# The last message pass of a four-layer graph network: VectorE's adds and scans in another order, marks of going-on destinations made once

## The chip, the cores and the metric

One core of one Trainium2 chip runs the whole kernel in one launch. The metric is the device time of a launch in microseconds (us), as the median of a few runs. Engines are named as the profile names them: PE is TensorE (PEld its weight loads), DVE is VectorE, ACT is ScalarE, POOL is GpSimd, SP is SyncE, which issues most DMAs here.

## The reference, cut to what matters

Four graph layers run over the same 106,250 edges, sorted by destination, and 6,250 nodes of 128 features; a layernorm follows each. The change lies in the last layer, an attention whose softmax is taken per destination and per feature:

```
a = f_src[src] + f_dst[dst]
e = where(a >= 0, a, 0.2 * a)
seg_max = segment_max(e, dst)                 # per destination and feature
ex = exp(e - seg_max[dst])
sa = ex / segment_sum(ex, dst)[dst]
rst = segment_sum(f_v[src] * sa, dst)
x = layernorm(x + rst)
```

## The kernel before

Nodes stand in 49 tiles of 128. Edges stand in chunks of 128; four chunks with the node tile that each goes to are a **group** (GROUP = 4, 512 edges), and there are 220 groups. `acc` holds, in SBUF, the sums of every node tile. Each layer is a pass over the groups (`edges0` to `edges3`), with node phases between (`after0` to `after3`). The change is in `edges3`.

A pass is a software pipeline written out by hand. `ps.run` takes a list of stages `(lag, function)`; step v runs, in the order of the list, each stage on group v - lag. Each stage puts its instructions on one engine, so the list's order is, engine by engine, the order in which that engine has to work them off. Between engines only semaphores order the work, and an engine that waits for one holds all that stands behind it.

What the stages of `edges3` do, for one group:

- SP: `load_far` and `near` loads, `load_resets`; POOL: `gather` (four indirect DMAs of source rows), `message(G)` (the product exp x value for the group's first chunk).
- ACT: `turn` (two activations, a 0/1 selector by node), `not_first` (L1399), `from_first` (L1406), `take` (L1426, logits out of PSUM), `shrinks` (L1465, L1469), `at_firsts` (L1476), `distance` and `at_zero` (L844, L852, the selector by edge), `exps` (L1513).
- PE: `below_top` (L1503, L1506: logits less the running top, turned), `spread_resets` (L1437: one row of 512 spread over 128 partitions into bank 6), `both_ends` (L1415, L1418), `factors` (L1483), then `sums_a` and `sums_b` (both L869): the four chunks' products into PSUM, chunk 0 in `sums_a`, chunks 1 to 3 in `sums_b`.
- DVE: `leaky` (L1430), `forward` (L1450) and `backward` (L1457), two scans along the 512 edges that make the top of each destination, `message(V)` (L1519, the product for chunks 1 to 3), `scaled` (L1494, the sums so far of a destination that goes on from the group before, multiplied by a factor), and four `add`s (L893) of PSUM into `acc`.

A destination can go on from one group to the next, with a higher top. `shrinks` makes the factor exp(-rise) for it, `at_firsts` puts it at the node's place in a row (the distance |node - first|, which is in `gap`, turned by a Relu), `factors` turns that on PE, and `scaled` multiplies: every node but the first is to keep its sum, which `others` says (0 at the first node, 1 elsewhere).

The waits that matter here:

- `forward` waits for `s_r`, which `spread_resets` of the same group gives.
- `spread_resets` waits for `s_top` of the group before (its `backward`), since bank 6 is one.
- `sums_b` waits for `s_msg_v`, which `message(V)` gives, and for the `add`s of the group before.
- Each `add` waits for the one before it (a tile of `acc` can repeat), the first for `scaled`, and `backward` for `forward`.

Of the kernel before, what the change touches and what calls it, by code (L numbers as in the profile page):

```python
# [15 lines left out]
P = 128  # L16
# [24 lines left out]
STEP = 2.0 ** 106  # L41
# [13 lines left out]
ds = bass.ds  # L55
# [95 lines left out]
def build(nc, a):  # L151
    PE, V, A, G, SP = nc.tensor, nc.vector, nc.scalar, nc.gpsimd, nc.sync
# [3 lines left out]
    def dram(name, shape, dt=F32):  # L156
        return nc.dram_tensor(name, shape, dt).ap()
# [5 lines left out]
    near_d = dram("near_d", [ITEMS_PAD // GROUP, GROUP * (P + 1)])  # L163
# [15 lines left out]
    def sb(ctx, name, shape, dt=F32):  # L179
        return ctx.enter_context(nc.sbuf_tensor(name, shape, dt))  # L180
# [13 lines left out]
    node_iota = sb(root, "node_iota", [P, P])  # L194
    ones_col = sb(root, "ones_col", [P, 1])
    tile_of = sb(root, "tile_of", [1, ITEMS_PAD], I32)
    node_step = sb(root, "node_step", [P, 1])
    banks = root.enter_context(nc.psum_tensor("banks", [P, 8, 512], F32))
    bank = [banks[:, i, :] for i in range(8)]
# [1119 lines left out]
    def edges3():  # L1319
# [8 lines left out]
        with Phase(nc, "e3") as ctx:  # L1328
            ps = EdgePass(ctx, fsv_t, 2 * D, W3, sels=2, turns=1)
# [3 lines left out]
            resets = ps.sb("resets", [1, 2, EDGES], BF16)  # L1333
            ones_row = ps.sb("ones_row", [1, P], BF16)
            top = ps.sb("top", [P, SPAN, EDGES])
            gap = ps.sb("gap", [P, SPAN, P])
            rise, shrink = ps.sb("rise", [P, 1]), ps.sb("shrink", [P, 2])
            at_first = ps.sb("at_first", [P, 2, P])
            others = ps.sb("others", [P, ROUND])
            minus, minus_node = ps.sb("minus", [P, P]), ps.sb("minus_node", [P, 1])  # L1340
            apart = ps.sb("apart", [P, GROUP, P])
            s_resets, s_far = ([ps.sem(f"{n}{u}") for u in range(2)] for n in ("resets", "far"))
            s_a, s_taken, s_l, s_r, s_run, s_top, s_d, s_exp, s_msg_g, s_msg_v = (
                ps.sem(n) for n in ("a", "taken", "l", "r", "run", "top", "d", "exp", "msg_g", "msg_v"))
            s_apart, s_gap, s_rise, s_shrink, s_first, s_f, s_others, s_scaled, start = (
                ps.sem(n) for n in ("apart", "gap", "rise", "shrink", "first", "f", "others", "scaled", "start"))
            B_A, B_D, B_R, B_F = (2, 3), (4, 5), 6, 7
            by_node = ByNode(ps, s_a, 2)
            distance, at_zero = ps.selector()
# [3 lines left out]
            V.tensor_scalar(minus_node[:], node_step[:], -1.0 / STEP, None, ALU.mult).then_inc(start, 1)  # L1353
            for e in (V, A, PE):
                e.wait_ge(start, 4)

            def gather(g):
                if g.old(2):
                    SP.wait_ge(s_others, g.upto(-2))
                by_node.load(g, s_gap)  # L1360
                ps.gather(g, ps.s_sums[-1])

            def load_far(g):
# [10 lines left out]
                    SP.wait_ge(s_r, g.upto(-2))  # L1374
                SP.dma_start(resets[:, g.r2, :], reset_d[ds(g.n, 1), :]).then_inc(s_resets[g.r2], 16)

            def first(g):

                return by_node.near[:, g.r2, 0, 1:2]

            def turn(g):

                by_node.here(A, g)
                if g.old(1):
                    A.wait_ge(by_node.s_t, g.upto(-1))
                A.activation(apart[:], by_node.near[:, g.r2, :, 1:], ACT.Abs, bias=minus_node[:], scale=1.0 / STEP
                             ).then_inc(s_apart, 1)
                A.wait_ge(s_apart, g.upto(0))
                if g.old(2):
                    A.wait_ge(s_a, g.upto(-2))  # L1390
                    A.wait_ge(s_others, g.upto(-2))
                A.activation(by_node.sel_t[:, g.r2], apart[:], ACT.Relu, bias=ones_col[:], scale=-1.0
                             ).then_inc(by_node.s_t, 1)

            def not_first(g):
                A.wait_ge(by_node.s_t, g.upto(0))
                if g.old(ROUND):
                    A.wait_ge(s_scaled, g.upto(-ROUND))
                A.activation(others[:, g.at(ROUND):g.at(ROUND) + 1], by_node.sel_t[:, g.r2, 0, 0:1], ACT.Identity,  # L1399
                             bias=ones_col[:], scale=-1.0).then_inc(s_others, 1)  # L1400

            def from_first(g):
                by_node.here(A, g)
                if g.old(SPAN):
                    A.wait_ge(s_first, g.upto(-SPAN))
                A.activation(gap[:, g.at(SPAN), :], node_iota[:], ACT.Abs, bias=first(g), scale=-STEP).then_inc(s_gap, 1)  # L1406

            def both_ends(g):
                ps.have_rows(PE, g)
# [59 lines left out]
                A.activation(shrink[:, g.r2:g.r2 + 1], rise[:], ACT.Exp, scale=-1.0).then_inc(s_shrink, 1)  # L1469

            def at_firsts(g):
                A.wait_ge(s_gap, g.upto(0))
                A.wait_ge(s_shrink, g.upto(0))
                if g.old(2):
                    A.wait_ge(s_f, g.upto(-2))
                A.activation(at_first[:, g.r2, :], gap[:, g.at(SPAN), :], ACT.Relu, bias=shrink[:, g.r2:g.r2 + 1],  # L1476
                             scale=-1.0).then_inc(s_first, 1)

            def factors(g):
                PE.wait_ge(s_first, g.upto(0))  # L1480
# [4 lines left out]
            def scaled(g):  # L1485
                ps.tiles_to = ps.tiles(g, DVE_ENGINE)
                V.wait_ge(s_f, g.upto(0))
                V.wait_ge(s_others, g.upto(0))
                if g.old(1):
                    V.wait_ge(ps.s_added[GROUP - 1], g.upto(-1))  # L1490
                else:
                    V.wait_ge(ps.zeroed, 1)
                to = acc[:, ds(ps.tiles_to[0], 1), 0:W3].rearrange("p a (k d) -> p (a k) d", k=2)
                V.scalar_tensor_tensor(out=to, in0=bank[B_F][:, 0:D].unsqueeze(1).to_broadcast([P, 2, D]),  # L1494
                                       scalar=others[:, g.at(ROUND):g.at(ROUND) + 1], in1=to, op0=ALU.add, op1=ALU.mult
                                       ).then_inc(s_scaled, 1)

            def below_top(g):
# [16 lines left out]
            def message(engine, s_msg, items):  # L1515
                def stage(g):
                    engine.wait_ge(s_exp, g.upto(0))
                    values = ps.row(g)[:, items, D:2 * D]
                    engine.tensor_tensor(values, values, ps.row(g)[:, items, 0:D], ALU.mult).then_inc(s_msg, 1)  # L1519
                return stage  # L1520
# [6 lines left out]
            def sums_b(g):  # L1527
                PE.wait_ge(s_msg_v, g.upto(0))
                ps.scatter(g, lambda i: [(0, ps.row(g)[:, i, :])], (1, 2, 3))

            ps.run([(0, gather), (0, load_far), (1, load_resets), (5, message(G, s_msg_g, slice(0, 1))),
                    (4, below_top), (3, spread_resets), (1, both_ends), (5, factors), (5, sums_a), (5, sums_b),
                    (5, distance), (2, take), (5, shrinks), (0, turn), (0, not_first), (1, from_first), (5, at_firsts),
                    (5, at_zero), (4, exps),
                    (2, leaky), (6, scaled), (6, ps.add(0, s_scaled)), (6, ps.add(1)), (6, ps.add(2)),
                    (5, message(V, s_msg_v, slice(1, 4))), (6, ps.add(3)), (3, forward), (3, backward)])

    with root:
        project0()
        edges0()  # L1540
        after0()
        edges1()
        after1()
        edges2()
        after2()
        edges3()
        after3()
# [48 lines left out]
```

## Time and profile before

| what | value |
|---|---|
| median of three runs | 5310.63 us (5308.48 to 5311.12) |
| the profiled execution, its own time | 5308.46 us |
| its span in the trace | 5306.7 us |
| busy: PE, DVE, ACT, POOL | 69%, 69%, 55%, 68% of the span |
| mean granted clock of TensorE | 0.85 of full speed |

The busy shares are means over four passes of different limits. The last pass runs from about 3846 us to 5205 us of the span, and only there do DVE, ACT and PE all stand near nine tenths. A time in a row of the timeline is that from the span's start; a duration of an instruction is from its start to its last write, so two that follow each other on DVE can overlap a little. The idle time in brackets is the engine's own before that instruction.

### The profile page before, as it was taken

To read this page: it belongs to the slowest core of one execution; us is meant where nothing else is said; L and a number is where in the kernel's file an instruction comes from. 1 tells how busy PE (TensorE), PEld (TensorE's weight loads), DVE (VectorE), ACT (ScalarE), POOL (GpSimd) and SP (SyncE) were. 2 spreads that over 40 slices of the span, in tenths; PEclk is the share of its full clock that TensorE was granted. 3 is DMA by queue.
4 is the path that set the end of the run, shared out by engine and by line. 5 is a ranking of instruction groups with operands and counts; after the bars stand their busy time and mean duration, and the time that the engine had idled before them with its cause. 6 is when DMAs were issued, how large, how long until landed. Compare 5 with 4: busy or idle time off the path is not lost. (4 is left out here: it accounts for less than half of the span.)

```text
span 5306.7 us, 96549 instructions
## 1 busy us (share of the span) xinstructions
PE 3639.6 (69%) x20063; PEld 3004.1 (57%) x20064; DVE 3680.0 (69%) x8656; ACT 2909.3 (55%) x7558; POOL 3627.0 (68%) x3835
## 2 busy tenths in 40 slices
PE   6444444451766666666678888888778888888882
PEld 4444444441655555555466666666567777777771
DVE  5666666667644444445577777777679999999997
ACT  2444444443522222224566666666479998989893
POOL 4777777773777777774477777777067777777772
PEclk7778877775877777777788988898989999999996
DMA  7444444442423333331111111111166666666661
GB/s 193 146 159 153 152 152 152 154 160 68 110 77 78 79 78 78 77 77 39 51 55 55 55 55 55 55 55 55 51 170 175 175 176 174 174 175 173 173 175 36
DMA packets 490311, 596.75 MB, mean 112 GB/s; under 512 B 126676, under 2 KB 348358, under 8 KB 489832
## 3 DMA queue, kind: packets, MB, share of 16 engines
q0 software_dynamic: 141696, 349.47, 23.6%
q1 hardware_dynamic: 347656, 245.85, 16.1%
q8 instruction: 32, 0.52, 0.0%
q10 hardware_dynamic: 864, 0.39, 0.0%
q14 instruction: 63, 0.52, 0.0%
HBM read 505.89 MB, written 30.07 MB: 101 GB/s over the span
## 5 line engine op out<-in xcount | busy, mean ns | idle before, releaser
L893 DVE TENSOR_TENSOR acc<-acc,banks 128x256 f32 (+1 forms) x3520 | 1359.9, 386 | 760.1 <-PE banks L869 500.8
L808 POOL DMA_INDIRECT e_rows<-kv_t,e_index x800 | 785.4, 982 | 243.7 <-issue 242.4
L808 POOL DMA_INDIRECT e_rows<-fsv_t,e_index x800 | 775.6, 970 | 257.8 <-issue 257.8
L808 POOL DMA_INDIRECT e_rows<-x_t,e_index x800 | 778.7, 973 | 249.7 <-issue 239.9
L808 POOL DMA_INDIRECT e_rows<-up_t,e_index x800 | 777.3, 972 | 243.8 <-issue 238.3
L869 PE MATMUL banks<-e_rows,e_sel 128*128 128x256 f32 x3520 | 920.6, 408 | 22.9 <-issue 14.7
L844 ACT ACTIVATE e_away<-node_iota,local 128x128 f32<-128x128 f32 x2640 | 840.3, 389 | 8.0 <-issue 1.0
L869 PE MATMUL banks<-e_msg,e_sel 128*128 128x137 f32 (+1 forms) x3520 | 762.2, 366 | 9.9 <-DVE acc L893 4.5
L869 PEld LDWEIGHTS banks<-e_rows,e_sel 128*128 128x128 f32 x3520 | 683.9, 205 | 136.4 <-issue 38.3
L970 PE MATMUL banks<-acc,e_sel_t 128*128 x1760 | 315.1, 335 | 580.6 <-DVE e_sel_t L937 566.3
L1095 ACT ACTIVATE e_rows<-banks,e_rows 128x128 f32<-128x128 f32 x880 | 250.0, 369 | 800.1 <-PE banks L1086 387.7
L869 PEld LDWEIGHTS banks<-e_msg,e_sel 128*128 128x128 f32 x3520 | 628.8, 220 | 60.9 <-DVE acc L893 5.0
L970 PEld LDWEIGHTS banks<-acc,e_sel_t 128*128 128x128 f32 x1760 | 274.0, 237 | 617.4 <-issue 616.5
L1086 PE MATMUL banks<-e_w,e_attr 65*128 65x128 f32 x1760 | 291.9, 319 | 398.1 <-DMA e_attr<-in_attr_rows 398.1
L1086 PEld LDWEIGHTS banks<-e_w,e_attr 65*128 65x128 f32 x1760 | 279.8, 231 | 432.0 <-issue 376.6
L852 ACT ACTIVATE e_sel<-e_away,ones_col 128x512 f32<-128x512 f32 x660 | 473.1, 717 | 20.9
L999 ACT ACTIVATE e_msg<-e_clip 128x32 f32<-128x32 f32 x220 | 51.1, 232 | 659.6 <-DVE e_clip L995 648.7
L937 DVE TENSOR_SCALAR e_sel_t<-e_near,node_step 128x512 f32<-128x512 f32 x220 | 113.1, 514 | 319.4 <-DMA e_near<-near_d 319.4
L1221 PE MATMUL banks<-e_emb,e_w 16*128 16x256 f32 x440 | 164.7, 457 | 181.3 <-DMA e_emb<-emb_d 161.8
L1457 DVE TENSOR_TENSOR_SCAN e_top<-banks,e_top 128x511 f32<-128x511 f32 x220 | 281.7, 1280 | 7.8
L1450 DVE TENSOR_TENSOR_SCAN e_top<-banks,e_top,e_logit 128x512 f32<-128x512 f32 x220 | 280.5, 1275 | 0.3 <-issue 0.3
L1252 PEld LDWEIGHTS banks<-e_w,e_h 65*128 65x128 f32 x1760 | 259.6, 212 | 18.2 <-issue 3.8
(202 smaller groups left out, 6637.1 us busy)
## 6 DMA issues: line engine op xcount, KB each, us to landing
e_near<-near_d SPq DMA_DIRECT2D x440, 258.0 KB, 4.2
e_far<-acc SPq DMA_DIRECT2D x880, 64.0 KB
e_attr<-in_attr_rows SPq DMA_DIRECT2D x880, 32.0 KB
e_rows<-kv_t,e_index POOLq DMA_INDIRECT x800
e_rows<-x_t,e_index POOLq DMA_INDIRECT x800
e_rows<-up_t,e_index POOLq DMA_INDIRECT x800, 2.5
e_rows<-fsv_t,e_index POOLq DMA_INDIRECT x800
kv_t<-proj_kv SPq DMA_DIRECT2D x12, 512.0 KB, 4.8
```

The source lines that it names most:

```text
L808: G.indirect_dma_start(out=self.rows[:, u, i, 0:self.width], out_offset=None, in_=self.table, in_offset=bass.IndirectOffsetOnAxis(ap=index ...
L844: m = A.activation(away[:, i, :], node_iota[:], ACT.Abs, bias=local[:, ds(g.n * GROUP + i, 1)], scale=-1.0)
L852: A.activation(self.place_of_sel(g), away[:], ACT.Relu, bias=ones_col[:], scale=-1.0).then_inc(self.s_sel, 1)
L869: m = PE.matmul(bank[n_bank][:, col + at:col + at + rows.shape[1]], self.place_of_sel(g)[:, i, :], rows, start=True, stop=True)
L893: V.tensor_tensor(to, to, bank[n_bank][:, col:col + self.sums].unsqueeze(1), ALU.add).then_inc(self.s_added[i], 1)
L970: m = PE.matmul(bank[B_Q[g.r2]][:, i * P:(i + 1) * P], by_node.sel_t[:, g.r2, i, :], side(ds(tiles[i], 1)).rearrange("p a d -> p (a d)"), ...
L1086: m = PE.matmul(bank[B_H[g.r2]][:, i * P:(i + 1) * P], attr[:, g.at(SPAN), i, :], w1[:], start=True, stop=True)
L1095: m = A.activation(ps.row(g)[:, i, D + 1:], bank[B_H[g.r2]][:, i * P:(i + 1) * P], ACT.Relu, scale=ps.row(g)[:, i, 0:1])
L1221: PE.matmul(hidden_bank(g, 0), w0[:], emb[:, g.at(SPAN), :], start=True, stop=True).then_inc(s_h1, 1)
L1252: m = PE.matmul(bank[B_W[g.r2]][:, i * P:(i + 1) * P], h2[:, g.r2, i * P:(i + 1) * P], w2[:], start=True, stop=True)
L1450: V.tensor_tensor_scan(top[:, g.at(SPAN), :], bank[B_R], logit[:, g.at(SPAN), :], top_before(g), ALU.add, ALU.max).then_inc(s_run, 1)
L1457: V.tensor_tensor_scan(back, bank[B_R][:, EDGES - 1:0:-1], back, top[:, g.at(SPAN), EDGES - 1:EDGES], ALU.add, ALU.max).then_inc(s_top, 1)
```

## The change

- The list of stages is reordered for DVE. `forward`, `backward` and `message(V)` move relative to the `add`s, and `leaky` moves behind the scans. ACT's and POOL's lists keep their order apart from what is taken out; PE's and SP's keep it.
- `shrinks` works one lag earlier (4 for 5).
- `not_first`, `from_first` and the ACT operation of `at_firsts` go. `at_firsts` becomes one DVE operation: is_equal of the node's number with the group's first destination, times the factor.
- `firsts` and `others` are made once for all 220 groups, before the first step: one DMA of 220 numbers, a cast, one matmul that spreads them, two DVE operations.
- The loads of `near` wait for `s_apart` instead of `s_gap` and `s_others`.

```
-            gap = ps.sb("gap", [P, SPAN, P])
-            others = ps.sb("others", [P, ROUND])
+            firsts, others = ps.sb("firsts", [P, N_GROUPS]), ps.sb("others", [P, N_GROUPS])
...
+                SP.dma_start(first_row[:], near_d[0:N_GROUPS, 1:2].rearrange("g a -> a g")).then_inc(s_heads, 16)
+            V.wait_ge(s_heads, 16)
+            V.tensor_copy(first_b[:], first_row[:]).then_inc(start, 1)
+            PE.wait_ge(start, 5)
+            PE.matmul(bank[B_F][:, 0:N_GROUPS], ones_row[:], first_b[:], start=True, stop=True).then_inc(spread_heads, 1)
+            V.wait_ge(spread_heads, 1)
+            V.tensor_scalar(firsts[:], bank[B_F][:, 0:N_GROUPS], 1.0 / STEP, None, ALU.mult).then_inc(start, 1)
+            V.tensor_scalar(others[:], bank[B_F][:, 0:N_GROUPS], node_step[:], None, ALU.not_equal).then_inc(start, 1)
+            V.wait_ge(start, 7)
+            PE.wait_ge(start, 7)
...
-                if g.old(2):
-                    SP.wait_ge(s_others, g.upto(-2))
-                by_node.load(g, s_gap)
+                by_node.load(g, s_apart)
...
             def at_firsts(g):
-                A.wait_ge(s_gap, g.upto(0))
-                A.wait_ge(s_shrink, g.upto(0))
+                V.wait_ge(s_shrink, g.upto(0))
                 if g.old(2):
-                    A.wait_ge(s_f, g.upto(-2))
-                A.activation(at_first[:, g.r2, :], gap[:, g.at(SPAN), :], ACT.Relu, bias=shrink[:, g.r2:g.r2 + 1],
-                             scale=-1.0).then_inc(s_first, 1)
+                    V.wait_ge(s_f, g.upto(-2))
+                V.tensor_scalar(at_first[:, g.r2, :], node_iota[:], firsts[:, ds(g.n, 1)], shrink[:, g.r2:g.r2 + 1],
+                                ALU.is_equal, ALU.mult).then_inc(s_first, 1)
...
                     (4, below_top), (3, spread_resets), (1, both_ends), (5, factors), (5, sums_a), (5, sums_b),
-                    (5, distance), (2, take), (5, shrinks), (0, turn), (0, not_first), (1, from_first), (5, at_firsts),
-                    (5, at_zero), (4, exps),
-                    (2, leaky), (6, scaled), (6, ps.add(0, s_scaled)), (6, ps.add(1)), (6, ps.add(2)),
-                    (5, message(V, s_msg_v, slice(1, 4))), (6, ps.add(3)), (3, forward), (3, backward)])
+                    (5, distance), (2, take), (4, shrinks), (0, turn), (5, at_zero), (4, exps),
+                    (6, scaled), (5, at_firsts), (6, ps.add(0, s_scaled)), (3, forward), (6, ps.add(1)), (3, backward),
+                    (6, ps.add(2)), (2, leaky), (6, ps.add(3)), (5, message(V, s_msg_v, slice(1, 4)))])
```

DVE, kernel before, one step from one `forward` (L1450) to the next, with no ends of the unrolled loop in it; the names show the scans as SCALAR_TENSOR_TENSOR:

```order
L1457 SCALAR_TENSOR_TENSOR e_top<-banks,e_top 128x511
L1430 SCALAR_TENSOR_TENSOR e_logit<-banks,e_logit 128x512
L898 TENSOR_LOAD tile_of
L1494 ISA
L1494 SCALAR_TENSOR_TENSOR acc<-banks,e_others,acc 128x256
L893 TENSOR_TENSOR acc<-acc,banks 128x256
L893 ISA
L893 TENSOR_TENSOR acc<-acc,banks 128x256
L893 ISA
L893 TENSOR_TENSOR acc<-acc,banks 128x256
L1519 TENSOR_TENSOR e_rows<-e_rows 128x3x128
```

DVE, kernel of the change, the stretch from `message(V)` (now L1510) of one step to the scans of the next (`forward` is now L1441, `backward` L1448, `scaled` L1485, `at_firsts` L1468):

```order
L1510 TENSOR_TENSOR e_rows<-e_rows 128x3x128
L898 ISA
L898 TENSOR_LOAD tile_of
L1485 ISA
L1485 SCALAR_TENSOR_TENSOR acc<-banks,e_others,acc 128x256
L1468 ISA
L1468 TENSOR_SCALAR e_at_first<-node_iota,e_firsts,e_shrink 128x128
L893 TENSOR_TENSOR acc<-acc,banks 128x256
L1441 SCALAR_TENSOR_TENSOR e_top<-banks,e_top,e_logit 128x512
L893 ISA
L893 TENSOR_TENSOR acc<-acc,banks 128x256
L1448 SCALAR_TENSOR_TENSOR e_top<-banks,e_top 128x511
```

`message(V)` stood two places ahead of `forward` of its own step (one `add` between). It is now the last of its step, behind both scans of that step, and `forward` of the next step is the fourth operation behind it.

PE, kernel of the change, from the sums of one step (L869) to those of the next; `below_top` is now L1494 and L1497, `spread_resets` L1428, `both_ends` L1406 and L1409, `factors` L1475:

```order
L869 MATMUL banks<-e_rows,e_sel 128x256 x4
L1494 MATMUL banks<-ident,e_logit 128x128 x4
L1497 MATMUL banks<-e_minus,e_top 128x128 x4
L1425 REGISTER_ALU
L1428 MATMUL banks<-e_resets,e_ones_row 128x512
L1401 REGISTER_ALU
L1402 ISA
L1406 MATMUL banks<-ident,e_rows 128x128 x4
L1409 MATMUL banks<-e_sel_t,e_far 128x128 x4
L1475 MATMUL banks<-ident,e_at_first 128x128
L869 MATMUL banks<-e_rows,e_sel 128x256 x4
```

PE's order is that of before, with other line numbers: nothing moved on it.

## Rows read from the trace of the kernel before

**Rows 1.** Stretch: length, busy PE, PEld, DVE, ACT, POOL; granted clock, DMA share, GB/s

```profile
4900.00:5100.00 200.00, 176.68 (x1125) 142.63 (x1124) 182.31 (x298) 180.33 (x465) 144.23 (x166) 1.00 0.64 174
```

**Rows 2.** Timeline of DVE, one step: start, us, engine, line, operation [idle before]

```profile
4499.68 1.28 DVE L1450 TENSOR_TENSOR_SCAN e_top<-banks,e_top,e_logit 128x512 f32<-128x512 f32 x1
4500.99 1.28 DVE L1457 TENSOR_TENSOR_SCAN e_top<-banks,e_top 128x511 f32<-128x511 f32 x1
4502.18 0.66 DVE L1430 SCALAR_TENSOR_TENSOR e_logit<-banks,e_logit 128x512 f32<-128x512 f32 x1
4502.77 0.47 DVE L1494 SCALAR_TENSOR_TENSOR acc<-banks,e_others,acc 128x256 f32 x1
4503.34 0.98 DVE L893 TENSOR_TENSOR acc<-acc,banks 128x256 f32 x2
4504.54 0.42 DVE L893 TENSOR_TENSOR acc<-acc,banks 128x256 f32 x1 [0.21 <-DVE acc L893]
4504.88 0.55 DVE L1519 TENSOR_TENSOR e_rows<-e_rows 128x384 f32<-128x384 f32 x1
4505.34 0.41 DVE L893 TENSOR_TENSOR acc<-acc,banks 128x256 f32 x1
4505.68 1.28 DVE L1450 TENSOR_TENSOR_SCAN e_top<-banks,e_top,e_logit 128x512 f32<-128x512 f32 x1
```

**Rows 3.** Instructions of line 1450 in the window 3900 to 5100 us

```profile
L1450 DVE TENSOR_TENSOR_SCAN e_top<-banks,e_top,e_logit x199: 1269/1276/1279, 3900.6 to 5099.6; 128x512 f32<-128x512 f32 x199
```

**Rows 4.** Timeline of PE in the same step

```profile
4502.32 0.66 PE L1503 MATMUL banks<-ident,e_logit 128*128 128x128 f32 x4 [0.81 <-DVE e_top L1457]
...
4503.81 0.39 PE L1437 MATMUL banks<-e_resets,e_ones_row 1*128 1x512 bf16 x1
...
4505.73 1.10 PE L869 MATMUL banks<-e_rows,e_sel 128*128 128x256 f32 x4
```

**Rows 5.** Timeline near the pass's end, where the sums wait for the message

```profile
5196.08 0.58 DVE L1519 TENSOR_TENSOR e_rows<-e_rows 128x384 f32<-128x384 f32 x1
...
5196.71 1.56 PE L869 MATMUL banks<-e_rows,e_sel 128*128 128x256 f32 x6 [0.36 <-DVE e_rows L1519]
```

**Rows 6.** Timeline near the pass's start, where a scan waits for the resets

```profile
3894.15 0.39 PE L1437 MATMUL banks<-e_resets,e_ones_row 1*128 1x512 bf16 x1
...
3894.63 1.28 DVE L1450 TENSOR_TENSOR_SCAN e_top<-banks,e_top,e_logit 128x512 f32<-128x512 f32 x1 [0.28 <-issue]
```

**Rows 7.** Timeline of PE in other passes: idle gaps of several lengths

```profile
895.10 1.15 PE L970 MATMUL banks<-acc,e_sel_t 128*128 x8 [1.78 <-DVE e_sel_t L937]
...
1431.86 1.68 PE L1086 MATMUL banks<-e_w,e_attr 65*128 65x128 f32 x8 [2.44 <-DMA e_attr<-in_attr_rows]
...
1436.25 1.06 PE L1086 MATMUL banks<-e_w,e_attr 65*128 65x128 f32 x8
...
1438.87 1.06 PE L1086 MATMUL banks<-e_w,e_attr 65*128 65x128 f32 x8
...
2461.21 0.66 PE L450 MATMUL banks<-ident,after_h 128*128 128x128 f32 x4 [2.42 <-DVE after_h L651]
...
3082.76 0.66 PE L1221 MATMUL banks<-e_emb,e_w 16*128 16x256 f32 x2 [3.00 <-DMA e_emb<-emb_d]
```

**Rows 8.** Stretches behind two of these gaps, columns as in the first group

```profile
1432.40:1435.60 3.20, 3.20 (x12) 2.75 (x11) 0.21 (x1) 1.14 (x4) 2.29 (x4) 0.50 0.32 86
...
3084.40:3087.70 3.30, 3.30 (x11) 2.78 (x11) 1.47 (x5) 2.43 (x7) 2.38 (x4) 0.50 0.14 42
```

**Rows 9.** Groups of instructions in the window 3900 to 5100 us: POOL, busy and mean ns, idle before

```profile
L808 POOL DMA_INDIRECT e_rows<-fsv_t,e_index x748 | 725.6, 970 | 240.8 <-issue 240.8
...
L1519 POOL TENSOR_TENSOR e_rows<-e_rows 128x128 f32<-128x128 f32 x199 | 91.1, 458 | 86.6 <-ACT e_rows L1513 85.2
```

**Rows 10.** Timeline of the pass's preparation

```profile
3859.92 0.15 DVE L1352 TENSOR_SCALAR e_minus<-ident 128x128 f32<-128x128 f32 x1
...
3861.89 1.09 PE L1415 MATMUL banks<-ident,e_rows 128*128 128x128 f32 x4 [20.27 <-DMA e_rows<-fsv_t,src]
```

More of the change, by code:

```diff
@@ L1335, in edges3 @@
             top = ps.sb("top", [P, SPAN, EDGES])
-            gap = ps.sb("gap", [P, SPAN, P])
             rise, shrink = ps.sb("rise", [P, 1]), ps.sb("shrink", [P, 2])
             at_first = ps.sb("at_first", [P, 2, P])
-            others = ps.sb("others", [P, ROUND])
+            firsts, others = ps.sb("firsts", [P, N_GROUPS]), ps.sb("others", [P, N_GROUPS])
+            first_row = ps.sb("first_row", [1, N_GROUPS])
+            first_b = ps.sb("first_b", [1, N_GROUPS], BF16)
             minus, minus_node = ps.sb("minus", [P, P]), ps.sb("minus_node", [P, 1])
@@ L1344, in edges3 @@
                 ps.sem(n) for n in ("a", "taken", "l", "r", "run", "top", "d", "exp", "msg_g", "msg_v"))
-            s_apart, s_gap, s_rise, s_shrink, s_first, s_f, s_others, s_scaled, start = (
-                ps.sem(n) for n in ("apart", "gap", "rise", "shrink", "first", "f", "others", "scaled", "start"))
+            s_apart, s_rise, s_shrink, s_first, s_f, s_scaled, start, s_heads, spread_heads = (
+                ps.sem(n) for n in ("apart", "rise", "shrink", "first", "f", "scaled", "start", "heads", "spread_heads"))
             B_A, B_D, B_R, B_F = (2, 3), (4, 5), 6, 7
@@ L1355, in edges3 @@
                 e.wait_ge(start, 4)
+            with nc.allow_non_contiguous_dma(reason="one number of each group, once"):
+                SP.dma_start(first_row[:], near_d[0:N_GROUPS, 1:2].rearrange("g a -> a g")).then_inc(s_heads, 16)
[8 more added lines that the diff above has]
+            PE.wait_ge(start, 7)
             def gather(g):
-                if g.old(2):
-                    SP.wait_ge(s_others, g.upto(-2))
-                by_node.load(g, s_gap)
+                by_node.load(g, s_apart)
                 ps.gather(g, ps.s_sums[-1])
@@ L1375, in load_resets @@
                 SP.dma_start(resets[:, g.r2, :], reset_d[ds(g.n, 1), :]).then_inc(s_resets[g.r2], 16)
-            def first(g):
-                return by_node.near[:, g.r2, 0, 1:2]
             def turn(g):
@@ L1390, in turn @@
                     A.wait_ge(s_a, g.upto(-2))
-                    A.wait_ge(s_others, g.upto(-2))
                 A.activation(by_node.sel_t[:, g.r2], apart[:], ACT.Relu, bias=ones_col[:], scale=-1.0
                              ).then_inc(by_node.s_t, 1)
[L1395 to L1406, printed above, removed]
             def both_ends(g):
@@ L1487, in scaled @@
                 V.wait_ge(s_f, g.upto(0))
-                V.wait_ge(s_others, g.upto(0))
                 if g.old(1):
@@ L1494, in scaled @@
                 V.scalar_tensor_tensor(out=to, in0=bank[B_F][:, 0:D].unsqueeze(1).to_broadcast([P, 2, D]),
-                                       scalar=others[:, g.at(ROUND):g.at(ROUND) + 1], in1=to, op0=ALU.add, op1=ALU.mult
+                                       scalar=others[:, ds(g.n, 1)], in1=to, op0=ALU.add, op1=ALU.mult
                                        ).then_inc(s_scaled, 1)
```

## The prediction, as it was put on record

> **What bounds the kernel now.** I read the page first: the four passes have different limits, and the change touches only the last. There the windows show DVE busy 91% of the time, ACT 90%, PE 88%, POOL 72%, and TensorE at its upper level of 2.4 GHz, granted clock 1.00 [rows 1]. So I read one step on DVE. Its nine operations follow each other with next to no idle time: from `forward` at 4499.68 to the next at 4505.68 is 6.00 us [rows 2], and over 198 steps it is (5099.6 - 3900.6) / 198 = 6.056 us [rows 3]. DVE sets the step. PE waits for it once a step: 0.81 us for `backward` [rows 4].
>
> The reader is to see two kinds of spacing in [rows 2]. Where nothing waits, the next operation starts a little before the last one ends: `leaky` starts 1.19 us after a scan of 1.28 us, `scaled` 0.59 after `leaky` (0.66), `message(V)` 0.34 after an `add` (0.42), an `add` 0.46 after the message, a scan 0.34 after an `add`. Where an operation waits for the one before, it starts later: `scaled` to `add` 0.57 (0.40 would be 0.47 less the usual 0.07), the second `add` 0.56, the third 0.64, `backward` 1.31 after `forward`.
>
> **The change on DVE alone.** All those waits now have another operation between. The unchained spacings sum to two scans 2 x 1.19, `leaky` 0.59, `scaled` 0.40, four `add`s 4 x 0.34, message 0.46: 5.19 us. `at_firsts` is new on DVE; nearest row is a tensor_scalar of the same 128x128 in 0.15 us [rows 10], bounds 0.07 (spacing) and 0.42 (an `add`, twice as wide); I take 0.15. That is 5.34 us a step, 0.7 below today. ACT loses three small activations and was not the bound. All this would be a gain, if nothing else came in.
>
> **What comes in: the message now stands between PE and the scan.** PE's order has not changed: `sums_b` of step v, then `below_top`, then `spread_resets` of step v+1. `sums_b` waits for `message(V)` of step v, and `forward` of step v+1 waits for `spread_resets` of step v+1. Before, the message came ahead of both scans, so PE did this work while DVE scanned. Now the message is DVE's last operation of the step, `forward` is the fourth of the next, and everything PE does between lies in a closed loop with it:
>
> - Message end to the sums' start: 5196.08 + 0.58 = 5196.66 to 5196.71, 0.05 us [rows 5].
> - Chunks 1 to 3, six matmuls: six take 1.56 us from the first start to the last end [rows 5], four take 1.10 [rows 4], so starts are 0.46 / 2 = 0.23 apart and the last one lasts 0.41. `below_top` can start 6 x 0.23 = 1.38 us behind the first. They are six and not eight, as in [rows 5], since chunk 0 has been summed.
> - `below_top` to `spread_resets`: 4503.81 - 4502.32 = 1.49 [rows 4]. `s_top` has long been given, so it doesn't wait.
> - `spread_resets` 0.39, and from its end to the scan 3894.63 - 3894.54 = 0.09 [rows 6].
>
> These are 3.40 us on PE's side. On DVE's side from `forward` to the end of the message: scan 1.19, `add` 0.34, scan 1.19, `add` 0.34, `leaky` 0.59, `add` 0.34, and the message in full, 0.55: 4.54 us. `scaled`, `at_firsts` and the first `add` (about 0.9 us) lie in the 3.40 us in which DVE can't scan; so does their register work, and `at_firsts` costs nothing. The loop is 3.40 + 4.54 = **7.94 us**, 1.88 above 6.056.
>
> It holds from the first step with a message (5) to the last with a `forward` (222): 217 intervals. With PE at its upper level throughout, this is 5308.46 + 217 x 1.884 = 5717.3 us.
>
> **TensorE's clock.** PE now has one long gap a step, between `sums_a` (chunk 0) and the message. From `spread_resets` to the sums is 4505.73 - 4503.81 = 1.92 us [rows 4]; the first `add` pair must be in by then, 0.48 + 1.19 + 0.42 + 0.05 = 2.14 after `spread_resets` began; chunk 0 ends at 2.14 + 0.23 + 0.41 = 2.78; the message ends at 0.48 + 4.54 = 5.02, and PE starts at 5.07. The gap is **2.29 us**. What gaps do is in other passes. After 1.78 us PE runs eight matmuls in 1.15 us, at its usual pace; after 2.42 us four transposes take 0.66, as at full speed; after 2.44 us the clock falls to 0.50 (1.2 GHz) for a stretch, and after 3.00 us too [rows 7, 8]. So 2.29 lies where it goes either way. What a fall costs: behind the gap of 2.44 the next group of the same sixteen matmuls starts 1436.25 - 1431.86 = 4.39 us later, against 1438.87 - 1436.25 = 2.62, so 1.77 us [rows 7]. Here a part of the slow stretch can fall ahead of PE's 3.4 us of work in the loop, so I take 1.6. I went through PE's timeline for the gaps of the other passes: of four of 2.2 to 2.5 us that began at full clock, three were followed by a fall (all but that at 2461.21), all near 3.0 were, hardly one near 1.8. I take 6 steps in 10, bounds 0 and 10: 0.96 us a step. Step 8.90 us.
>
> The Trainium skill says (TensorE: Matmul & The Clock Gate, HAM oscillation) that bursts of matmuls with waits between can be throttled anew at every burst. By that rule every step would pay, which is rival 3; the gap of 2.42 us speaks against "every".
>
> **What I cost at nothing.** The preparation (DMA of 220 numbers, cast, matmul, two DVE operations, about 1 us behind 3860.1) lies ahead of PE's first matmul at 3861.89, which waits for other things [rows 10]; exposed it would be 1 to 3 us, once. The DMA lies under the clearing of `acc`. POOL needs 4 x (0.970 + 0.322) + 0.46 = 5.63 us a step [rows 9], under 8.9. ACT's 5.4 less 1.0 us too. The `near` loads wait for less than before.
>
> **The sum.** 5308.46 + 217 x (8.90 - 6.056) = 5308.46 + 617.1 = 5926 us. The profiled execution lies 2.2 us below the median: **5928 us**.
>
> **Rivals.**
>
> 1. The clock stays up in nearly all steps: 5720 us (0 of 10; 2 in 10 is 5789). For it: gaps of 1.8 and one of 2.42 that cost nothing. Against: three of four like ours. Chance 0.15.
> 2. The other side, faster: PE's sums and `below_top` don't hold back the scan, and DVE's 5.34 us comes to bear; then POOL's 5.63 is the bound, and 5308.46 + 217 x (5.65 - 6.056) = 5220 us. It decides where PE's side of the loop takes under 5.65 - 4.54 = 1.1 us; it takes 3.40, by rows. It can only be if I have the order of waits wrong. Chance 0.05.
> 3. Every step pays 1.77 us: 9.71 us a step, 6104. For it: a gap of 3.0 pays, and mine could be longer by some tenths. Chance 0.08.
> 4. DVE's operations don't overlap in the new order, so the stretch is 2 x 1.28 + 3 x 0.42 + 0.66 + 0.55 = 5.03 in place of 4.54: with the clock as in my forecast 217 x 0.49 = 106 more, 6034. In [rows 2] they overlap, after a scan too. Chance 0.05. The Trainium skill says (VectorE: DVE Perf Modes, The DRAIN you can't avoid) that an operation doesn't start until the pipe of the last is empty and that a semaphore in between costs nothing extra. By it alternation buys nothing. The trace differs: 0.34 us unchained against 0.56 to 0.64 chained.
> 5. No change that shows: the loop closes but is hidden. With 3.40 us of PE work and no other group's scan to put there, I find no way. Chance 0.02.
>
> **How the numbers follow.** My forecast has 0.60, with its own range 5835 to 6020 (4 to 8 falls in 10 steps give 5858 to 5997 by 1.6 us each, and 0.1 us a step on the loop is 22). The remaining 0.05 is for sums beyond all this. The range 5715 to 6025 adds most of rival 1 and some of 4: about 0.8. A measurement of this kernel tells 0.2% (11 us) from nothing. Slower 0.93, same 0.02, faster 0.05.
>
> **What would show it.** In the trace of the changed kernel: steps of 8 to 10 us; DVE idle about 2.4 us or more ahead of `forward`, released by PE's `spread_resets`; PE idle some 2.3 us ahead of L869, released by DVE's message; six matmuls of L869 straight behind the message's end; granted clock in the pass below 1.00, in stretches of 0.50; POOL and ACT less busy. I am wrong in the mechanism if DVE doesn't wait ahead of `forward`, and in a size if the steps are near 7.94 (no falls) or near 9.7.

## The result, and the profile after

| | before | changed |
|---|---|---|
| median | 5310.41 us | 5911.68 us (5909.21 to 5915.28, 4 runs) |
| profiled execution | 5308.46 us | 5910.12 us |
| granted clock, mean of the span | 0.85 | 0.83 |

The change makes the kernel slower: ratio 1.1133, 95% interval 1.1114 to 1.1153. The forecast was 5928 us in a range from 5715 to 6025.

Busy time by engine, from the page of the kernel before and from that of the changed one. DVE's busy time grows by 12 us and PE's by 231 (about the same number of matmuls, part of them at the lower clock); the span is 601 us longer:

```profile
PE 3639.6 (69%) x20063; PEld 3004.1 (57%) x20064; DVE 3680.0 (69%) x8656; ACT 2909.3 (55%) x7558; POOL 3627.0 (68%) x3835
...
PE 3870.7 (66%) x20064; PEld 3162.5 (54%) x20065; DVE 3692.0 (62%) x8879; ACT 2790.9 (47%) x6898; POOL 3626.9 (61%) x3835
```

A stretch of the last pass of the changed kernel, columns as in [rows 1]. No engine is at its limit any more, and the clock is no longer 1.00:

```profile
4500.00:4700.00 200.00, 144.69 (x759) 114.31 (x758) 126.15 (x228) 110.73 (x247) 97.74 (x113) 0.88 0.45 121
```

The instructions of `forward` (now line 1441) in the window 4000 to 5600 us: durations, first and last start, and what its engine waited for ahead of it:

```profile
L1441 DVE TENSOR_TENSOR_SCAN e_top<-banks,e_top,e_logit x181: 1282/1282/1284, 4002.1 to 5596.7; 128x512 f32<-128x512 f32 x181
its engine sat idle before it (us, times) until:
  PE banks L1428: 569.5, 181
```

The step is (5596.7 - 4002.1) / 180 = 8.859 us, where [rows 3] gave 6.056. DVE waits ahead of every one of the 181 scans, 3.15 us on average, and what ends the wait is always L1428, `spread_resets`.

The timeline of DVE in the changed kernel, a short step and the end of the next, a long one. Line 1448 is `backward`, 1421 `leaky`, 1510 the message, 1485 `scaled`, 1468 `at_firsts`:

```profile
3896.54 1.28 DVE L1441 TENSOR_TENSOR_SCAN e_top<-banks,e_top,e_logit 128x512 f32<-128x512 f32 x1 [3.80 <-PE banks L1428]
3897.74 0.40 DVE L893 TENSOR_TENSOR acc<-acc,banks 128x256 f32 x1
3898.05 1.27 DVE L1448 TENSOR_TENSOR_SCAN e_top<-banks,e_top 128x511 f32<-128x511 f32 x1
3899.24 0.40 DVE L893 TENSOR_TENSOR acc<-acc,banks 128x256 f32 x1
3899.55 0.68 DVE L1421 SCALAR_TENSOR_TENSOR e_logit<-banks,e_logit 128x512 f32<-128x512 f32 x1
3900.15 0.41 DVE L893 TENSOR_TENSOR acc<-acc,banks 128x256 f32 x1
3900.48 0.55 DVE L1510 TENSOR_TENSOR e_rows<-e_rows 128x384 f32<-128x384 f32 x1
3900.95 0.48 DVE L1485 SCALAR_TENSOR_TENSOR acc<-banks,e_others,acc 128x256 f32 x1
3901.34 0.34 DVE L1468 TENSOR_SCALAR e_at_first<-node_iota,e_firsts,e_shrink 128x128 f32<-128x128 f32 x1
3901.82 0.42 DVE L893 TENSOR_TENSOR acc<-acc,banks 128x256 f32 x1
3904.39 1.28 DVE L1441 TENSOR_TENSOR_SCAN e_top<-banks,e_top,e_logit 128x512 f32<-128x512 f32 x1 [2.14 <-PE banks L1428]
...
3913.90 1.28 DVE L1441 TENSOR_TENSOR_SCAN e_top<-banks,e_top,e_logit 128x512 f32<-128x512 f32 x1 [3.81 <-PE banks L1428]
```

What [rows 2] showed as chained spacings of 0.56 to 0.64 us between `add`s is gone: from `forward` to the message's end is 3901.03 - 3896.54 = 4.49 us. But behind the first `add` DVE is idle for 2.14 us in the short step (3904.39 - 3896.54 = 7.85 us) and for 3.81 in the long one (9.51 us). Counted over the pass, 129 of the 219 steps are long ones of 9.3 us or more. Every tenth step, at an end of the unrolled loop, takes 0.4 us more than its kind (8.24 us for 7.85), so the mean of short steps is 7.89.

PE in the same kernel, a slow and a fast passage of the same work. L869 are the sums, 1494 and 1497 `below_top`, 1428 `spread_resets`:

```profile
4706.96 1.62 PE L869 MATMUL banks<-e_rows,e_sel 128*128 128x256 f32 x6 [2.14 <-DVE e_rows L1510]
4708.37 1.06 PE L1494 MATMUL banks<-ident,e_logit 128*128 128x128 f32 x4
4709.22 1.92 PE L1497 MATMUL banks<-e_minus,e_top 128*128 128x128 f32 x8
4711.07 0.60 PE L1428 MATMUL banks<-e_resets,e_ones_row 1*128 1x512 bf16 x1
...
4713.51 0.67 PE L869 MATMUL banks<-e_rows,e_sel 128*128 128x256 f32 x2 [0.20 <-DVE acc L893]
4716.31 1.56 PE L869 MATMUL banks<-e_rows,e_sel 128*128 128x256 f32 x6 [2.14 <-DVE e_rows L1510]
4717.72 0.60 PE L1494 MATMUL banks<-ident,e_logit 128*128 128x128 f32 x4
4718.15 1.06 PE L1497 MATMUL banks<-e_minus,e_top 128*128 128x128 f32 x8
4719.14 0.38 PE L1428 MATMUL banks<-e_resets,e_ones_row 1*128 1x512 bf16 x1
```

And the clock in these two passages:

```profile
4716.40:4719.50 3.10, 3.10 (x20) 2.55 (x20) 1.07 (x3) 1.94 (x4) 0.94 (x1) 1.00 0.58 159
...
4708.20:4711.00 2.80, 2.80 (x14) 2.55 (x12) 0.00 (x0) 0.19 (x1) 0.78 (x1) 0.52 0.33 94
```

The reader is to see the loop closing: six matmuls of the sums wait for the message (L1510), `below_top` and `spread_resets` follow, then the scan. Each time PE has been idle 2.14 us before. In the one passage the clock is at its lower level from `below_top` on (0.52: nearly all at 1.2 GHz), some 1.2 us after PE took up work again; in the other it isn't.

### The profile page after: what moved, and what is told of

The parts are those of the page before. It is cut to its first block and busy times, and to the rows that moved or that the text cites. A ratio compares the mean times of both kernels' runs of the same rounds, so it can differ in the third digit from the quotient of the medians.

```text
span 5908.1 us, 95632 instructions
## 1 busy us (share of the span) xinstructions
PE 3870.7 (66%) x20064; PEld 3162.5 (54%) x20065; DVE 3692.0 (62%) x8879; ACT 2790.9 (47%) x6898; POOL 3626.9 (61%) x3835
## 5 line engine op out<-in xcount | busy, mean ns | idle before, releaser
L869 PE MATMUL banks<-e_rows,e_sel 128*128 128x256 f32 x3520 | 1042.5, 435 | 532.8 <-DVE e_rows L1510 462.4
L869 PEld LDWEIGHTS banks<-e_rows,e_sel 128*128 128x128 f32 x3520 | 687.1, 210 | 750.4 <-DVE e_rows L1510 549.9
L869 PE MATMUL banks<-e_msg,e_sel 128*128 128x137 f32 (+1 forms) x3520 | 763.5, 366 | 10.0 <-DVE acc L893 4.6
L1441 DVE TENSOR_TENSOR_SCAN e_top<-banks,e_top,e_logit 128x512 f32<-128x512 f32 x220 | 282.2, 1283 | 686.6 <-PE banks L1428 685.6
L869 PEld LDWEIGHTS banks<-e_msg,e_sel 128*128 128x128 f32 x3520 | 627.8, 219 | 61.2 <-DVE acc L893 5.0
L1510 POOL TENSOR_TENSOR e_rows<-e_rows 128x128 f32<-128x128 f32 x220 | 100.8, 458 | 730.3 <-ACT e_rows L1504 730.3
L1504 ACT ACTIVATE e_rows<-banks 128x512 f32<-128x512 f32 x220 | 131.5, 598 | 481.8 <-PE banks L1497 481.8
L1497 PE MATMUL banks<-e_minus,e_top 128*128 128x128 f32 x1760 | 323.6, 346 | 0.0
```

Of the source, the lines that this page charges most:

```text
L869: m = PE.matmul(bank[n_bank][:, col + at:col + at + rows.shape[1]], self.place_of_sel(g)[:, i, :], rows, start=True, stop=True)
L1441: V.tensor_tensor_scan(top[:, g.at(SPAN), :], bank[B_R], logit[:, g.at(SPAN), :], top_before(g), ALU.add, ALU.max).then_inc(s_run, 1)
L1497: m = PE.matmul(bank[B_D[g.r2]][:, i * P:(i + 1) * P], top[:, g.at(SPAN), i * P:(i + 1) * P], minus[:], start=False, stop=(i == GROUP - 1))
L1504: A.activation(ps.row(g)[:, :, 0:D], quad(B_D[g.r2]), ACT.Exp).then_inc(s_exp, 1)
```

## The experiments

The theory was: a closed loop message, sums, `below_top`, `spread_resets`, `forward`, and back to the message, of 7.9 us; and on top of it TensorE's clock, which falls behind PE's long gap in some 6 steps of 10. Rivals: the parts other than the order (marks, `at_firsts`, the semaphore of the `near` loads) carry some of it; the long steps have another cause; alternation buys nothing.

Below, "before" is always the kernel before, timed on the same chip in the same rounds: 5319.0 us in the first set (experiments 1 to 4), 5316.3 in the second, 5317.1 in the third. The changed kernel was timed beside a "before" of 5310.4, so a difference between it and an experiment can be some 9 us off; the ratios aren't. Steps are taken as above, from the first and last start of the scan in the window 4000 to 5000 us; in it the kernel before has 6.045 us, the changed one 8.87.

### 1. The order alone

The kernel before, and only this:

```
-                    (2, leaky), (6, scaled), (6, ps.add(0, s_scaled)), (6, ps.add(1)), (6, ps.add(2)),
-                    (5, message(V, s_msg_v, slice(1, 4))), (6, ps.add(3)), (3, forward), (3, backward)])
+                    (6, scaled), (6, ps.add(0, s_scaled)), (3, forward), (6, ps.add(1)), (3, backward),
+                    (6, ps.add(2)), (2, leaky), (6, ps.add(3)), (5, message(V, s_msg_v, slice(1, 4)))])
```

> The kernel before with nothing but DVE's list in the changed order (ACT keeps its marks and factors). My theory, a loop from the message (last on DVE) through PE's sums and below_top to spread_resets and the next forward: the loop doesn't hold any of the removed ACT work or at_firsts, so the whole slowdown is here, steps in two kinds of about 7.9 and 9.5 us, 5890 to 5925 us. Rival, the new parts (at_firsts on DVE, preparation, near loads under another semaphore) carry a part of it: under 5850 us.

Measured 5917.3 us, ratio 1.1126 (1.1108 to 1.1145), step 8.83 us. Within the 0.2% of the interval the whole slowdown is the order; marks and factors carry none of it that shows.

### 2. The loop made shorter

The changed kernel with `spread_resets` ahead of `below_top` in PE's list:

```
-                    (4, below_top), (3, spread_resets), (1, both_ends), (5, factors), (5, sums_a), (5, sums_b),
+                    (3, spread_resets), (4, below_top), (1, both_ends), (5, factors), (5, sums_a), (5, sums_b),
```

> The changed kernel with spread_resets ahead of below_top in PE's list. My theory: the loop loses the 1.49 us of below_top and is about 6.4 us (7.85, the short step of the changed kernel, less 1.49), and PE's gap shrinks to about 1 us, so the clock stays at 1.00: 5308 + 217 x (6.4 - 6.05) = 5384, 5365 to 5420 us. Rival, the wait is that of the message on something else, or the clock falls for another reason than the gap: steps stay near 7.9 to 8.9 us, over 5650.

Measured 5417.5 us, ratio 1.0182 (1.0165 to 1.0199). The scan's row in the window 4000 to 5000 us gives (4994.5 - 4003.4) / 151 = 6.564 us a step:

```profile
L1441 DVE TENSOR_TENSOR_SCAN e_top<-banks,e_top,e_logit x152: 1282/1283/1284, 4003.4 to 4994.5; 128x512 f32<-128x512 f32 x152
...
4500.00:4700.00 200.00, 160.00 (x1038) 127.46 (x1039) 169.41 (x304) 142.06 (x333) 135.85 (x153) 1.00 0.60 160
```

The loop lost 1.3 us where 1.49 was expected (1.42 by the changed kernel's own rows); the scan still waits for PE. The gap is shorter (1.29 us in the timeline), and the clock is back at 1.00. So one edit on PE takes away the clock's term and most of the loop's at once; experiment 4 separates them.

### 3. The loop cut

The changed kernel with `spread_resets` one lag earlier, so that the next step's `forward` finds its resets there:

```
-                    (4, below_top), (3, spread_resets), (1, both_ends), (5, factors), (5, sums_a), (5, sums_b),
+                    (4, below_top), (1, both_ends), (5, factors), (5, sums_a), (2, spread_resets), (5, sums_b),
```

> The changed kernel with spread_resets one lag earlier (2 for 3), between sums_a and sums_b in PE's list: it then waits for the backward of its own step and is done before the message. My theory: the loop is cut, DVE's own operations (about 5.5 us a step) or POOL (5.63) bound, no gap of PE over 1 us, clock 1.00: steps of 5.6 to 5.8 us, 5210 to 5255 us, faster than before. Rival A, chained operations cost DVE nothing and their alternation buys nothing: steps of 6.0 us or more, 5300 or more. Rival B, another loop behind this one takes over: between 5255 and 5700.

Measured 5214.3 us, ratio 0.9801 (0.9785 to 0.9817): faster than before, and 697 us faster than the changed kernel by moving one matmul. The timeline, DVE and PE around the message:

```profile
4503.32 0.39 PE L1428 MATMUL banks<-e_resets,e_ones_row 1*128 1x512 bf16 x1
...
4503.63 0.56 DVE L1510 TENSOR_TENSOR e_rows<-e_rows 128x384 f32<-128x384 f32 x1
...
4504.24 1.56 PE L869 MATMUL banks<-e_rows,e_sel 128*128 128x256 f32 x6 [0.54 <-DVE e_rows L1510]
...
4504.49 0.34 DVE L1468 TENSOR_SCALAR e_at_first<-node_iota,e_firsts,e_shrink 128x128 f32<-128x128 f32 x1
4504.98 0.42 DVE L893 TENSOR_TENSOR acc<-acc,banks 128x256 f32 x1
4505.31 1.28 DVE L1441 TENSOR_TENSOR_SCAN e_top<-banks,e_top,e_logit 128x512 f32<-128x512 f32 x1
```

`spread_resets` is done before the message, and the scan starts 0.33 us behind the `add`, with no wait. PE is idle 0.54 us ahead of these sums, and the step is 5.64 us. Alternation does buy something: rival A falls.

### 4. The gap filled

The changed kernel with idle matmuls in PE's gap; the loop is as it was:

```
+            def fill(g):
+                for _ in range(3):
+                    PE.matmul(bank[B_D[g.r2]][:, 0:2 * P], ident[:], w_sdv[:, 0:2 * P], start=True, stop=True)
...
-                    (4, below_top), (3, spread_resets), (1, both_ends), (5, factors), (5, sums_a), (5, sums_b),
+                    (4, below_top), (3, spread_resets), (1, both_ends), (5, factors), (5, sums_a), (5, fill), (5, sums_b),
```

> The changed kernel with three idle products of 128x256 (six PE matmuls, about 1.4 us) between sums_a and sums_b, into a bank that nothing reads then: PE works through most of the gap, the result is unused. The work is added on PE and none is taken away. My theory, two terms, loop and clock: the clock stays at 1.00 and every step is the short one, 7.85 us: 5308 + 217 x (7.85 - 6.05) = 5699, 5685 to 5730 us. Rival, the long steps come of something else than the clock (DMA, ACT): no faster than the changed kernel, 5900 or more.

Measured 5705.8 us, ratio 1.0727 (1.0709 to 1.0745). More work on PE makes the changed kernel 206 us faster. The scan's row and the window 4000 to 5000 us:

```profile
L1441 DVE TENSOR_TENSOR_SCAN e_top<-banks,e_top,e_logit x127: 1282/1283/1285, 4004.0 to 4998.4; 128x512 f32<-128x512 f32 x127
...
4000.00:5000.00 1000.00, 857.05 (x5072) 690.31 (x5072) 705.19 (x1266) 623.53 (x1395) 544.26 (x634) 1.00 0.50 133
```

The step is 7.89 us, the clock 1.00 in this window, and of PE's gap 0.85 us are left. So of the changed kernel's 601 us some 206 to 216 are the clock (by the medians, and by the ratios 1.1133 and 1.0727) and the other 385 to 395 the loop, which this run shows alone.

### 5. A fifth of the gap filled

As above with `range(1)` in place of `range(3)`.

> As the variant with the filled gap, with one idle product of 128x256 in place of three: two PE matmuls, 0.46 us of the gap of about 2.14 us are filled, 1.7 are left. The work is added on PE. By the gaps of 1.78 us in the trace of before, after which the clock hardly ever fell, my theory expects few falls and nearly all steps at 7.85: 5690 to 5750 us. Rival, the share of falls goes down in proportion to the gap: 4 to 5 in 10 steps, 5830 to 5880.

Measured 5833.4 us, ratio 1.0973 (1.0956 to 1.0989). Here I was wrong, and the time is the rival's, though not its 4 to 5 long steps in 10. Scan, window, and one slow passage:

```profile
L1441 DVE TENSOR_TENSOR_SCAN e_top<-banks,e_top,e_logit x119: 1282/1283/1285, 4001.9 to 4995.2; 128x512 f32<-128x512 f32 x119
...
4000.00:5000.00 1000.00, 762.91 (x4280) 602.83 (x4279) 662.29 (x1189) 583.71 (x1307) 511.91 (x596) 0.94 0.46 125
...
4709.02 2.76 PE L869 MATMUL banks<-e_rows,e_sel 128*128 128x256 f32 x6 [1.71 <-DVE e_rows L1510]
```

The gap is 1.71 us, as worked out, and the step 8.42 us. Counted, 74 of its 219 steps are long, against 129 of 219 with the gap of 2.14 us. The means say the same: with 7.89 for a short step and 1.66 more for a long one (9.51 - 7.85), (8.42 - 7.89) / 1.66 = 3.2 in 10 and (8.87 - 7.89) / 1.66 = 5.9 in 10. So no one length of gap decides: with 2.14 us in every step the clock falls in some and not in others, and it falls more rarely with 1.71. The gaps of 1.78 us in [rows 7] were a poor guide. There they came once in some 50 us (895.10, the next at 946.70), here one comes in every step; that this is why was not tried. Nor do these runs separate the gap's length from how much of the step PE works, since both changed together.

### 6. The parts alone

The changed kernel with DVE's list in the old order, `at_firsts` between `scaled` and the first `add`:

> The changed kernel with DVE's list back in the order of before (at_firsts between scaled and the first add): marks made once and at_firsts on DVE, no alternation. My theory: DVE bounds and carries one operation more, 0.88 us from scaled to the first add (as in the kernel with early resets) for 0.57 before: steps of about 6.3 us, 1.0 to 1.4% slower than before. Rival, the ACT work taken out is what matters: no slower than before.

```
+                    (2, leaky), (6, scaled), (5, at_firsts), (6, ps.add(0, s_scaled)), (6, ps.add(1)), (6, ps.add(2)),
+                    (5, message(V, s_msg_v, slice(1, 4))), (6, ps.add(3)), (3, forward), (3, backward)])
```

Measured 5305.9 us, ratio 0.9981 (0.9971 to 0.9991). I had expected it 1.0 to 1.4% slower: wrong. The timeline shows why:

```profile
4502.72 0.48 DVE L1485 SCALAR_TENSOR_TENSOR acc<-banks,e_others,acc 128x256 f32 x1
4503.11 0.34 DVE L1468 TENSOR_SCALAR e_at_first<-node_iota,e_firsts,e_shrink 128x128 f32<-128x128 f32 x1
4503.37 0.98 DVE L893 TENSOR_TENSOR acc<-acc,banks 128x256 f32 x2
...
3864.50 1.27 DVE L1441 TENSOR_TENSOR_SCAN e_top<-banks,e_top,e_logit 128x512 f32<-128x512 f32 x1
```

From `scaled` to the first `add` is 0.65 us, against 0.57 in [rows 2]: `at_firsts` sits in the time that the `add` waits anyway. The 0.49 us from `at_firsts` to the `add` in experiment 3, which I had taken for its cost, was the `add`'s wait for the sums of chunk 1, which start only when the message ends. The step is 6.08 us for 6.05, and what is gained lies at the pass's start: the first `forward` comes at 3864.50 us, at 3870.91 in the kernel before. Of these 6.4 us, 3.4 lie ahead of the pass already (`acc` is cleared from 3845.39 us on, for 3848.81, and between the profiled runs that time varies by 11 us); 3.0 are the pass's own, where ACT waits longer for the third `near` load in the kernel before, and 3.5 more come in the four steps behind.

### 7. The cut loop with the old parts

The kernel of experiment 1 with the edit of experiment 3.

> The kernel before with DVE's list in the changed order and spread_resets early (as in the fast variant), ACT keeping its marks and factors. My theory: alternation alone is the gain, DVE needs 5.1 us, POOL 5.63 and ACT about 5.6 bound: within 1% of the variant with the new parts (5214), 5200 to 5265 us. Rival, it needs the new parts, since ACT at nine tenths busy becomes the bound: over 5265.

Measured 5299.9 us, ratio 0.9963 (0.9950 to 0.9976), step 6.02 us. The rival was right. Window and waits of this kernel:

```profile
4000.00:5000.00 1000.00, 908.37 (x5652) 724.71 (x5651) 871.09 (x1496) 906.40 (x2327) 716.92 (x831) 1.00 0.66 175
...
DVE acc L893 <- PE banks L869: 128.1, 167, 1.7
...
PEld banks L1483 <- ACT e_at_first L1476: 65.5, 152, 1.2
```

ACT is busy 91%, PE waits for ACT's `at_first`, and DVE's `add` for PE's sums; that ACT is the limit is read from these waits. So the parts, which alone bring 0.2%, are worth 86 us (5300 to 5214) once DVE's chain is loosened.

### 8. The message early, PE's list untouched

The changed kernel, only DVE's list:

```
-                    (6, scaled), (5, at_firsts), (6, ps.add(0, s_scaled)), (3, forward), (6, ps.add(1)), (3, backward),
-                    (6, ps.add(2)), (2, leaky), (6, ps.add(3)), (5, message(V, s_msg_v, slice(1, 4)))])
+                    (6, scaled), (5, at_firsts), (6, ps.add(0, s_scaled)), (5, message(V, s_msg_v, slice(1, 4))),
+                    (6, ps.add(1)), (2, leaky), (6, ps.add(2)), (3, forward), (6, ps.add(3)), (3, backward)])
```

> The changed kernel, PE's list as it is, DVE's: scaled, at_firsts, add 0, message, add 1, leaky, add 2, forward, add 3, backward. The message is early again, so the loop through PE has over 2 us of slack, and adds and scans still alternate. My theory: DVE's own 5.6 us and POOL bound, clock 1.00: 5205 to 5240 us. Rival, the place of spread_resets itself, ahead of which PE waits for the backward scan, costs: over 5300.

Measured 5173.1 us, ratio 0.9735 (0.9705 to 0.9765), faster than the 5205 to 5240 that I expected and the best of all. The 5.6 us that I had taken for DVE's own work is experiment 3's step, the wait of its first `add` included. Run again with more rounds:

> The fastest variant again for a narrower interval: DVE is busy without a gap (5.40 us a step), so 2.4 to 2.9% faster than before.

Measured 5174.3 us (5162.55 to 5195.11), ratio 0.9732 (0.9711 to 0.9753). The window of the first of the two:

```profile
4000.00:5000.00 1000.00, 979.81 (x6307) 787.56 (x6305) 999.79 (x1855) 862.72 (x2042) 796.33 (x928) 1.00 0.73 196
```

DVE is busy 999.79 of 1000 us, at 5.39 us a step; PE 98%. POOL is busy 796 us, and 200 more stand idle behind its gathers, 0.27 us each, so it has next to no slack either.

### 9. Add 3 late

The changed kernel, message early, but the last `add` behind both scans:

```
+                    (6, scaled), (5, at_firsts), (6, ps.add(0, s_scaled)), (5, message(V, s_msg_v, slice(1, 4))),
+                    (6, ps.add(1)), (3, forward), (6, ps.add(2)), (3, backward), (6, ps.add(3)), (2, leaky)])
```

> The changed kernel, PE's list as it is, DVE's: scaled, at_firsts, add 0, message, add 1, forward, add 2, backward, add 3, leaky. The message is early, but add 3, for which sums_b waits ahead of chunks 2 and 3, comes behind both scans. My theory: a second loop by the same rule, from add 3 through four matmuls, below_top and spread_resets (0.05 + 0.92 + 1.42 + 0.38 + 0.10) to forward and back to the end of add 3 (1.20 + 0.31 + 1.19 + 0.41): 5.98 us, 5285 to 5320 us. Rival, only the message matters: as the kernel with the message early and add 3 ahead of backward, 5205 to 5240.

Measured 5306.9 us, ratio 0.9981 (0.9971 to 0.9990), step (4994.4 - 4000.0) / 164 = 6.063 us against 5.98 expected. The waits of this kernel name the second loop: PE's sums wait for DVE's `add`, and DVE's scan waits again:

```profile
PE banks L869 <- DVE acc L893: 137.1, 165, 1.2
...
DVE e_top L1441 <- issue: 82.0, 149, 0.6
DVE e_top L1441 <- PE banks L1428: 14.1, 15, 0.9
```

It has the same operations as experiment 8 in DVE's list, and costs 0.67 us a step more: what decides is what PE waits for, and how far ahead of `forward` it comes. (`leaky` stands elsewhere too; it wasn't moved alone.) (The wait ahead of the scan is put down to "issue" in most steps; that it is the one for `spread_resets` follows from the length that I had worked out, not from that row.)

### 10. The best order with the old parts

The kernel before with the list of experiment 8 (without `at_firsts`).

> The kernel before with DVE's list as in the fastest variant (message early, adds and scans alternating), ACT keeping marks and factors. After the run with the cut loop and the old parts, where ACT with its 5.45 us of work was the limit: I expect ACT again, steps of 5.85 to 6.05 us, 5265 to 5315 us. Rival, there it was the late message that made sums and adds late, and with the message early the order alone gives the whole gain: under 5230.

Measured 5300.3 us, ratio 0.9964 (0.9952 to 0.9976), step 5.98 us, ACT busy 91%. As in experiment 7: with the old parts the order gains 0.4%, wherever the message stands. By the waits ACT holds DVE back. Which of the parts weighs most (ACT's three operations, the lag of `shrinks`, the semaphore of the `near` loads) was not tried apart.

## Why the prediction was right, point by point

- **DVE bounds, in chained spacings.** Right. Experiment 8, where DVE never stands idle, needs 5.39 us; 5.34 was worked out, with 0.15 for `at_firsts`.
- **The loop of 7.94 us.** Measured 7.85 (short step), and 7.89 as a mean with the clock held up (experiment 4), which has the ends of the unrolled loop in it. On DVE's side 4.49 for 4.54. On PE's side 3.36 for 3.40: 0.05 to the sums, 1.41 and 1.42 between the starts, 0.38, and 0.10 to the scan.
- **217 steps.** 217 x (8.859 - 6.056) = 608 us; the profiled execution grew by 601.7. The 6 us between lie at the pass's ends, which I had counted as nothing. From the first `forward` to the last it is 603 us longer, the first comes 4 us earlier (3866.87 us for 3870.91), and behind the last it takes 2 us more. The 4 us are the order's too: the first scan comes 17.9 us after the clearing of `acc` starts, 17.95 in experiment 1 with the old parts, 22.1 in the kernel before, where the second `leaky` stands ahead of it.
- **The clock, 0.96 us a step.** The gap was 2.14 us for 2.29, the fall costs 9.51 - 7.85 = 1.66 for the 1.6 taken, and 129 of 219 steps pay it, 5.9 in 10, where 6 were taken. The share was chosen from four gaps and was lucky to be this near; the reason behind it, that gaps near 1.8 us don't count, experiment 5 showed to be wrong.
- **`at_firsts` 0.15 us.** Mis-sized: 0.34 us, from start to the next start 0.26 in experiment 6. It cost nothing here, as said.
- **POOL's bound of 5.63 us.** Wrong by a little: in experiment 8 the step is 5.39 with POOL busy 80%. The 0.32 us that stands idle behind each gather isn't there ahead of POOL's message, so it comes three times a step, and 0.16 us behind the message. By that run's own figures POOL needs 4 x 0.956 + 0.466 + 200.1 / 186 = 5.37 us, hardly less than DVE: as a bound it was mis-sized, not absent. It played no part in the forecast, only in rival 2, whose mechanism (the loop cut) experiment 3 made real, with 5.64 us a step and 5214 us for 5220; there DVE's waits set it and not POOL.
- **Rivals.** 1 (clock always up) is experiment 4, 5706 us for 5720. 3 (every step) is excluded by the two kinds of steps. The prediction tied it to the Trainium skill (TensorE: Matmul & The Clock Gate, HAM oscillation), and went further than the page: the waits in its example, after which every burst is slow, are longer than PE's here. With 2.14 us, 90 of 219 steps pay nothing. 4 (no overlap) is excluded by the 4.49 us on DVE; the section of the Trainium skill that it names (VectorE: DVE Perf Modes, The DRAIN you can't avoid) says itself that an operation that isn't held starts earlier, which the prediction left out and this trace bears out (an `add` starts 1.20 us after a scan of 1.28). 5 (nothing shows) is excluded by the 11%.

## What to carry to other kernels

In a software pipeline whose engines work their lists off in order, moving an operation on one engine moves where every other engine's queue stands: follow the closed path (the operation, what waits for it, all that is queued behind that waiter, back to the engine) and compare its length with the step. Here one operation moved from two places ahead of a scan to the end of the step made a path of 7.85 us out of one that was hidden; the same alternation with the message early is 2.7% faster than before. And PE, set waiting once a step, can lose clock as well: a gap of 2.1 us a step cost a third of the slowdown.

## What the runs showed of the hardware that I had not expected

**Filling PE's gap with useless matmuls made the kernel faster.** With PE idle 2.14 us (changed kernel), 1.71 (experiment 5), 1.29 (experiment 2) and 0.85 (experiment 4) in each step, the granted clock from 4000 to 5000 us was 0.88, 0.94, 1.00 and 1.00, and long steps were 129, 74, 0 and 0 of 219.

**DVE's product of SBUF tensors ran longer where it started while POOL's was running.** The same kernel (experiment 8) ran at 5.39 us a step in one profiled execution and at 5.53 in the other ((4995.9 - 4000.8) / 180), DVE without idle time in both. DVE's groups in the window 4000 to 5000 us, of the first and of the second:

```profile
L1510 DVE TENSOR_TENSOR e_rows<-e_rows 128x384 f32<-128x384 f32 x185 | 100.0, 541 | 0.0
```

```profile
L1510 DVE TENSOR_TENSOR e_rows<-e_rows 128x384 f32<-128x384 f32 x181 | 124.2, 686 | 0.0
```

And the second's timeline, where DVE's message starts 0.20 us behind POOL's:

```profile
4501.89 0.46 POOL L1510 TENSOR_TENSOR e_rows<-e_rows 128x128 f32<-128x128 f32 x1
4502.09 0.69 DVE L1510 TENSOR_TENSOR e_rows<-e_rows 128x384 f32<-128x384 f32 x1
4502.51 1.13 POOL L808 DMA_INDIRECT e_rows<-fsv_t,e_index  x1 [0.16 <-issue]
```

In the first, POOL's message started at 4503.46 and DVE's at 4504.87, 0.54 us long. All 181 messages of the second overlap with POOL's in this way, none of the 185 of the first does. An overlap alone isn't enough, though. In experiment 6 POOL's message often starts while DVE's is running, and DVE's keeps its 0.55 us:

```profile
4608.27 0.55 DVE L1510 TENSOR_TENSOR e_rows<-e_rows 128x384 f32<-128x384 f32 x1
4608.70 0.46 POOL L1510 TENSOR_TENSOR e_rows<-e_rows 128x128 f32<-128x128 f32 x1 [0.55 <-ACT e_rows L1504]
```

DVE's message, 0.145 us longer, would by itself make the difference of 0.14 us a step. But on POOL, where the message isn't longer, the gather behind it is, 1.13 us for 0.99, which is 0.14 as well, and POOL has no more slack than DVE. Which of the two sets the 5.53 us stays open, and so does the cause, which is read from these rows; no run set the overlap apart.
